# Layer 1 of two graph layers: three places for h, values of two tiles ago beside the transposes, source product over tanh, mask in two pieces

## The reference, cut to what matters

```python
h = jnp.einsum('bnd,ade->bane', feat_in, W)            # 12 heads of 64
th = jnp.tanh(h)
attn_src = jnp.einsum('bane,aeo->bano', th, w_src)
attn_dst = jnp.einsum('bane,aeo->bano', th, w_dst)
attn = attn_src + jnp.swapaxes(attn_dst, 2, 3)
attn = jnp.where(attn >= 0, attn, LEAKY_ALPHA * attn)
attn = jnp.where(~adj[:, None, :, :], jnp.float32(-999.0), attn)
attn = jax.nn.softmax(attn, axis=-1)
feat_out = jnp.einsum('banm,bame->bane', attn, h) + b
feat_out = jax.nn.elu(feat_out)                        # heads side by side
gate = jax.nn.sigmoid(feat_in @ H_w.T + H_b)
return gate * feat_out + (1.0 - gate) * feat_in        # then x + this, layernorm
```

## Time and profile before

| | us |
|---|---|
| median of 3 runs | 2741.1 |
| lowest, highest | 2740.21, 2742.04 |
| the profiled execution | 2743.32 |
| its span | 2741.6 |
| TensorE busy in the span | 2720.1 |
| VectorE busy | 1676.8 |
| ScalarE busy | 1211.7 |
| GpSimd busy | 926.6 |

### The profile page before, as it was taken

The page is one execution under the profiler, slowest core; times in us unless marked ns, Lnnn a source line. Parts: engine busy times, 40 slices in busy tenths (PEclk is TensorE's granted clock), DMA queues, the critical chain, the costliest instruction groups (busy, mean ns, idle before and its releaser), DMA issues.

```text
span 2741.6 us, 51890 instructions
## 1 busy us (share of the span) xinstructions
PE 2720.1 (99%) x20988; PEld 2513.6 (92%) x20988; DVE 1676.8 (61%) x3335; ACT 1211.7 (44%) x3109; POOL 926.6 (34%) x566
## 2 busy tenths in 40 slices
PE   8999999999999999999999999999999999999998
PEld 7777778878888899999999999999999999999998
DVE  7899998888888764444444444444544444444443
ACT  5666676666666743233332333233332333233332
POOL 2353334434444223323332333323332333323330
PEclk9999999999999999999999999999999999999999
DMA  6655665555555522222222222222232222222220
GB/s 186 171 137 145 164 158 143 140 140 140 137 141 139 189 65 67 73 82 71 59 82 70 72 69 67 73 82 71 59 82 71 80 61 68 73 82 71 59 70 24
DMA packets 306896, 269.50 MB, mean 98 GB/s; under 512 B 227809, under 2 KB 244193, under 8 KB 306657
## 3 DMA queue, kind: packets, MB, share of 16 engines
q1 hardware_dynamic: 306656, 266.19, 35.5%
HBM read 142.65 MB, written 75.89 MB: 80 GB/s over the span
## 4 chain that ended last, share of the span: by engine, by line
PE 88%; DVE 5%; DMA 3%; issue 2%; ACT 2%; SPq 1%; POOL 0%; DVEq 0%; ACTq 0%; POOLq 0%
PE ps_hg L1069 21%; PE ps_k L70 15%; PE ps_a L70 15%; PE ps_q L70 15%; PE ps_a L1244 15%; PE ps_s L1185 2%; PE ps_c L1210 2%; PE ps_pv L1101 1%; DMA dst_all<-dst_scratch 1%; ACT logits L567 1%; PE ps_t L1088 1%; PE ps_pt L1210 1%; DMA dst_scratch<-dst 1%; PE ps_pt L1192 1%; DVE logits L792 1%
## 5 line engine op out<-in xcount | busy, mean ns | idle before, releaser
L1069 PE MATMUL ps_hg<-w_hi,xT 128*128 128x512 f32 x2268 | 745.6, 401 | 4.5 <-DVE h_one L825 4.2
L1069 PEld LDWEIGHTS ps_hg<-w_hi,xT 128*128 128x128 f32 x2268 | 426.2, 188 | 108.1 <-issue 6.7
L1069 PE MATMUL ps_hg<-w_lo,xT 128*128 128x512 f32 x1134 | 448.4, 395 | 0.0
L70 PE MATMUL ps_k<-x1T_hi,wk_hi 128*128 128x256 f32 x1152 | 329.0, 286 | 0.0
L70 PE MATMUL ps_k<-x1T_lo,wk_hi 128*128 128x256 f32 x1152 | 321.8, 279 | 0.0
L70 PE MATMUL ps_k<-x1T_hi,wk_lo 128*128 128x256 f32 x1152 | 321.1, 279 | 0.0
L70 PE MATMUL ps_q<-x1T_hi,wq_hi 128*128 128x256 f32 x1140 | 319.3, 280 | 0.0
L70 PE MATMUL ps_q<-x1T_lo,wq_hi 128*128 128x256 f32 x1140 | 318.5, 279 | 0.0
L70 PE MATMUL ps_q<-x1T_hi,wq_lo 128*128 128x256 f32 x1140 | 317.8, 279 | 0.0
L497 POOL TENSOR_TENSOR th_src<-th,wsrc_all 128x768 f32<-128x768 f32 x64 | 118.3, 1849 | 479.9 <-DVE dst_all L805 462.1
L657 ACT ACTIVATE qT<-ps_q,bq_col 128x256 f32<-128x256 f32 x192 | 80.5, 470 | 451.6 <-PE ps_q L70 451.6
(11 more groups left out here) (156 smaller groups left out, 5747.3 us busy)
## 6 DMA issues: line engine op xcount, KB each, us to landing
x_tok<-x SPq DMA_DIRECT2D x64, 384.0 KB, 4.1
dst_all<-dst_scratch SPq DMA_DIRECT2D x128, 192.0 KB, 3.4
gate_scratch<-gate SPq DMA_DIRECT2D x64, 384.0 KB, 2.6
feat_scratch<-feat SPq DMA_DIRECT2D x128, 192.0 KB, 2.8
feat_in<-feat_scratch SPq DMA_DIRECT2D x62, 384.0 KB, 3.1
gate_in<-gate_scratch SPq DMA_DIRECT2D x62, 384.0 KB, 3.7
x_even<-x SPq DMA_DIRECT2D x16, 768.0 KB, 4.2
x_odd<-x SPq DMA_DIRECT2D x16, 768.0 KB, 4.4
```

Of the source, the lines that this page charges most:

```text
L70: ins = pe.matmul(out, left[a][c], right[b][c], start=(n == 0), stop=(n == len(terms) - 1))
L1069: ins = pe.matmul(ps_hg[:, cols], left[a][c], right[b][c], start=(c == 0 and n == 0), stop=(c == KC - 1 and n == 2))
```

## The change

`h_one` gets a third place, taken by `T % 3`; it lies where `th_src` lay, and GpSimd writes the source product over `th` instead. So `tanh_h(T)` waits for the sum over that product of T-1 (`src_done`), and GpSimd's wait for the sum goes. On TensorE `values(T-2)` moves behind `project(2, T)`, ahead of `transpose_probs(T-1)`. `attention`, the two exp steps and `elu` run three tiles behind in place of two, at the same place of a tile, and so do the stores of feat; the hand-over takes in the one left over. Mask and maximum are made in two pieces: the four heads of VectorE before the wait for ScalarE's Prelu, the eight of ScalarE behind it. Some SBUF offsets move by 64 bytes or so; `ones` lies over `att`.

```diff
-        th_src = at(S + 24576, "th_src", [P, D])
+        h_hole = at(S + 24576, "h_hole", [P, HEADS0, EW])
...
-        h_one = at(S + 36864, "h_one", [P, 2, HEADS0, EW])
+        h_one = [at(S + 36928, "h_one0", [P, HEADS0, EW]), h_hole, at(S + 40064, "h_one2", [P, HEADS0, EW])]
...
-                if 2 <= T < NT - 1:
-                    store_feat(T - 2)
+                if 3 <= T < NT - 1:
+                    store_feat(T - 3)
...
+            sp.wait_ge(pv_done, NT - 2)
             feat_and_gate(1, 0)
             for n in range(EARLY_W1, EARLY_W1 + KC):
                 load_chunk(sp, w1_chunks[n], w1_in[n])
+            store_feat(NT - 4)
             store_feat(NT - 3)
...
-                if T >= 1:
-                    pool.wait_ge(src_done, T)
-                pool.tensor_tensor(th_src[:, :], th[:, :], wsrc_all[:, :], ALU.mult).then_inc(thsrc_done, 1)
+                pool.tensor_tensor(th[:, :], th[:, :], wsrc_all[:, :], ALU.mult).then_inc(thsrc_done, 1)
...
                     act.wait_ge(thdst_done, T)
-                    act.wait_ge(thsrc_done, T)
+                    act.wait_ge(src_done, T)
                 act.activation(th[:, :], ps_hg[:, 0:D], ACT.Tanh).then_inc(tanh_done, 1)
...
                 exp_scores(T - 1)
-                if T >= 2:
-                    elu_exp(T - 2)
+                if T >= 3:
+                    elu_exp(T - 3)
...
             copy_probs(NT - 2)
+            elu_exp(NT - 3)
             act.wait_ge(cols_in, 48)
...
+            def masked_max(T, part, first, last):
+                n = last - first
+                scores_ = per_head(logits[:, first * NODES:last * NODES], n)
+                dve.copy_predicated(
+                    scores_, not_adj[:, T % 2, :].unsqueeze(1).to_broadcast([P, n, NODES]),
+                    masked[:, 0:1].unsqueeze(2).to_broadcast([P, n, NODES])).then_inc(masked_done, 1)
+                dve.wait_ge(masked_done, 2 * T + part + 1)
+                dve.tensor_reduce(neg_max[:, first:last], scores_, AX_X, ALU.max, negate=True).then_inc(max_done, 1)
...
-                dve.wait_ge(prelu_done, T + 1)
                 dve.wait_ge(leaky_done, T + 1)
                 dve.wait_ge(mask_done, T + 1)
-                dve.copy_predicated(
...
+                masked_max(T, 0, ON_ACT, HEADS0)
+                dve.wait_ge(prelu_done, T + 1)
+                masked_max(T, 1, 0, ON_ACT)
+                dve.wait_ge(max_done, 2 * (T + 1))
...
-                if T >= 2:
-                    dve.wait_ge(pv_done, T - 1)
-                dve.tensor_tensor(h_one[:, T % 2, :, 0:E0], per_head(ps_hg[:, 0:D], HEADS0),
+                if T >= 3:
+                    dve.wait_ge(pv_done, T - 2)
+                dve.tensor_tensor(h_one[T % 3][:, :, 0:E0], per_head(ps_hg[:, 0:D], HEADS0),
...
-                if T >= 2:
-                    attention(T - 2)
+                if T >= 3:
+                    attention(T - 3)
                 if T > 2:
                     bias_h(T)
                 if T == NT - 1:
                     bias_g(T)
+                    elu(T - 3)
                     break
                 src_scores(T)
                 bias_g(T)
-                if T >= 2:
-                    elu(T - 2)
+                if T >= 3:
+                    elu(T - 3)
...
+            attention(NT - 3)
+            softmax_scores(NT - 1)
             elu(NT - 3)
-            softmax_scores(NT - 1)
             attention(NT - 2)
...
                 project(1, T).then_inc(h_done, 1)
+                project(2, T).then_inc(g_done, 1)
                 if T >= 2:
                     values(T - 2)
-                project(2, T).then_inc(g_done, 1)
                 if T >= 2:
                     transpose_probs(T - 1)
```

More of the change, by code:

```diff
@@ L151, in two_graph_layers @@
         th = at(S + 21504, "th", [P, D])
-        th_src = at(S + 24576, "th_src", [P, D])
-        ones = at(S + 24576, "ones", [P, P])
-        Hb_less1 = at(S + 27648, "Hb_less1", [P, D])
-        dst_all = at(S + 30720, "dst_all", [P, D])
+        h_hole = at(S + 24576, "h_hole", [P, HEADS0, EW])
+        Hb_less1 = at(S + 27712, "Hb_less1", [P, D])
+        dst_all = at(S + 30784, "dst_all", [P, D])
         th_dst = dst_all
-        logits = at(S + 33792, "logits", [P, D])
+        logits = at(S + 33856, "logits", [P, D])
         probs = logits
-        h_one = at(S + 36864, "h_one", [P, 2, HEADS0, EW])
[L160 to L171, removed]
+        h_one = [at(S + 36928, "h_one0", [P, HEADS0, EW]), h_hole, at(S + 40064, "h_one2", [P, HEADS0, EW])]
+        probsT = at(S + 43200, "probsT", [P, HEADS0, NODES])
+        att = at(S + 46272, "att", [P, D])
+        ones = at(S + 46272, "ones", [P, P])
+        feat = at(S + 49344, "feat", [P, D])
+        gate = at(S + 52416, "gate", [P, D])
+        adj_u8 = at(S + 55488, "adj_u8", [P, 4, NODES], U8)
+        not_adj = at(S + 55744, "not_adj", [P, 2, NODES], U8)
+        dst = at(S + 55872, "dst", [P, HEADS0])
+        src = at(S + 55936, "src", [P, 2, HEADS0])
+        neg_max = at(S + 56032, "neg_max", [P, HEADS0])
+        row_inv = at(S + 56096, "row_inv", [P, 2, HB])
+        masked = at(S + 56160, "masked", [P, 1])
+        b_less1 = at(S + 56192, "b_less1", [P, E0])
         x1T_hi = at(S, "x1T_hi", [P, KC, GN], F32R)
@@ L788, in softmax_scores @@
                                          op0=ALU.mult, op1=ALU.max).then_inc(leaky_done, 1)
-                dve.wait_ge(prelu_done, T + 1)
                 dve.wait_ge(leaky_done, T + 1)
                 dve.wait_ge(mask_done, T + 1)
-                dve.copy_predicated(
-                    per_head(logits[:, :], HEADS0),
-                    not_adj[:, T % 2, :].unsqueeze(1).to_broadcast([P, HEADS0, NODES]),
-                    masked[:, 0:1].unsqueeze(2).to_broadcast([P, HEADS0, NODES])).then_inc(masked_done, 1)
-                dve.wait_ge(masked_done, T + 1)
-                dve.tensor_reduce(neg_max[:, :], per_head(logits[:, :], HEADS0), AX_X, ALU.max,
-                                  negate=True).then_inc(max_done, 1)
-                dve.wait_ge(max_done, T + 1)
+                masked_max(T, 0, ON_ACT, HEADS0)
+                dve.wait_ge(prelu_done, T + 1)
+                masked_max(T, 1, 0, ON_ACT)
+                dve.wait_ge(max_done, 2 * (T + 1))
                 dve.tensor_tensor(per_head(logits[:, :], HEADS0), per_head(logits[:, :], HEADS0),
@@ L830, in src_scores @@
                 dve.wait_ge(thsrc_done, T + 1)
-                dve.tensor_reduce(src[:, T % 2, :], per_head(th_src[:, :], HEADS0), AX_X, ALU.add).then_inc(src_done, 1)
+                dve.tensor_reduce(src[:, T % 2, :], per_head(th[:, :], HEADS0), AX_X, ALU.add).then_inc(src_done, 1)
             def bias_g(T):
@@ L890, in _ @@
             dve.memset(masked[:, :], MASKED0).then_inc(fixed, 1)
-            dve.memset(h_one[:, :, :, E0:EW], 1.0).then_inc(fixed, 1)
+            for place in h_one:
+                dve.memset(place[:, :, E0:EW], 1.0).then_inc(fixed, 1)
             rest_x(0)
@@ L895, in _ @@
             dve.wait_ge(memsets, 2)
-            dve.wait_ge(fixed, 2)
+            dve.wait_ge(fixed, 4)
             bias_h(0)
@@ L1101, in values @@
                             ins = pe.matmul(ps_pv[graph(half), g, k * EW:(k + 1) * EW], probsT[graph(g), a, :],
-                                            h_one[graph(g), T % 2, a, :], start=True, stop=True)
+                                            h_one[T % 3][graph(g), a, :], start=True, stop=True)
                 ins.then_inc(pv_done, 1)
```

2 lines of the change are left out of this document (1 added, 1 removed).

## The result

The changed kernel takes 2753.9 us (median of five executions; 2753.2 to 2756.0) against 2741.1 for the kernel before (median of five too; 2740.2 to 2742.0): a ratio of 1.0048, with an interval of 1.0036 to 1.0059. It is slower by some 13 us, above the range of 2731.5 to 2744. The profiled execution took 2753.59 us with a span of 2751.9, so it too has 1.7 us around its span, and the spans can be compared: 2751.9 less 2741.6 is +10.3 us.

The account below looks back on a forecast made before the run. TensorE, busy 99% of the span, was taken to bound the kernel. Terms -2.5 + 0.5 - 0.7 - 1.4 + 0.6 = -3.5 us took the median from 2741.1 to 2737.6 us; range 2731.5 to 2744.

Parts of the forecast that it names:

- the hand-over: Layer 1 to layer 2: tile 61's attention, exp and elu move in, delaying last exp and transposes; +0.6 us, 0 to +1.5.
- slower: Outcome of a measurement over 2746.6 us, said to be most of rival 3; chance 0.07.
- First tiles: TensorE's two early waits for h_one shrink, the second replaced by some 0.55 us for att; -1.4 us, -2 to 0.
- The meeting: Values and transposes side by side on TensorE save 0.04 us a tile over 62 tiles; -2.5 us, -3 to -1.
- rival 2: TensorE gains nothing because both tiling-mode drains are kept, and stalls only move; 2741 us, chance 0.12.
- The new wait of the values: Values on TensorE now need att from the same tile, with 0.01 us of slack; +0.5 us, 0 to 3.
- Rival 3: att is late in every tile, so values wait in each; slower, 2747.5 us at 0.16 us a tile; chance 0.09.
- The turns: Late dst-to-mask chains in tiles 10 to 25, VectorE full or DMA late, stall TensorE less; -0.7 us, -3 to +3.
- The DMA-bound ones: Six turns late through DMA, 14.7 to 15.4 us long, shortened by 0.55 each; they leave stalls of 1.25 us.
- The pieces: Mask and max in two pieces on VectorE: chain 0.55 us shorter where it waited for Prelu, +0.3 where not.
- rival 4: Third h place does nothing, only the pieces count; 2739 us, inside the forecast's 0.52.
- The source product: GpSimd writes it over tanh, so the next tanh waits for src; 8.6 us of cover, cost 0.

Follow-up runs that it names:

- The first two experiments: Changed kernel with the store of tile 60's feat moved on SP: right behind the loop, 2743.05 us; only ahead of the six weight loads, 2746.28 us.
- the first experiment: Changed kernel with the store of tile 60's feat issued on SP right behind layer 1's loop, ahead of everything: 2743.05 us, 1.0005 of before.
- its own pair of kernels: Attention at tile's end, load of x behind dst's write: 2738.67 us; same with values back between second and third projection: 2741.30 us.
- the two kernels with x behind and attention in the middle: Load of x moved behind dst's write, in the kernel before: 2742.69 us; in the changed kernel with tile 60's store ahead of everything: 2745.22 us.

## Why the prediction was wrong

**The step that failed is the hand-over: +0.6, "ends 0 and +1.5", measured +11.8, of which the store's place in SP's queue made 10.6.** I looked at the waits of the instructions that move in, attention, exp and elu of tile 61, on VectorE and ScalarE, and priced their length. I also looked at SP, but only downward, at what stands behind the stores; I named x_g[1] and the weights. I did not look at what elu_exp(61) waits for. Its wait for feat_stored of tile 60 stands two lines under its head, and the diff itself shows `store_feat(NT - 4)` put behind the load_chunk loop. In the trace of before the six loads at that place (from 937.18) took 3.1 us to issue, and a store behind them was harmless. With the upper end of that term at +10 in place of +1.5, "slower" would have had more than 0.07. The first two experiments show the cause: 12.8, 3.6 and 1.2 us above the kernel before as the store moves forward, with waits of 9.3, 2.6 and 0.6 us. Of the rest of the stretch, +1.2 in the first experiment with 0.6 of it the wait for exp, the term as I had meant it was right.

**First tiles: -1.4, measured +1.8 in tiles 1 to 3.** In the first half tile 2's start came 0.88 us sooner, counted from tile 1's (13.25 us in place of 14.13), against the 0.55. That is luck: the kernel with the mask in one piece and the one with the source product alone have 13.25 us there too, so the pieces did not bring it. The second half had the wrong price. att ended at 68.45 and the values started at 68.59, 0.25 ahead of the old start of tile 4. But what used to be done before the wait, values and transposes, now stood behind it: 1.49 us at full clock (615.35 to 616.84 in tile 41) and 2.70 here (68.59 to 71.29). -0.25 + 2.70 is the +2.45 at tile 4. I had set 0.55 of waiting against 1.4 and left out the work behind it, and the clock, which stood at 0.53 in 69.00 to 72.00, behind a stop of 3 us. The chain in tile 3 did not come sooner by att and elu either, since ScalarE waited for the DMA and not for VectorE:

```profile
60.38 2.52 ACT L567 ACTIVATE logits<-dst_all,src 128x64 f32<-128x64 f32 x8 [2.64 <-DMA dst_all<-dst_scratch]
```

With attention at the tile's end this loss is gone (tile 4 starts at 67.44), which bears this out.

**The meeting: -2.5, measured -2.6** by its own pair of kernels, and 0.048 us a tile in the trace where 0.04 was forecast. Right, and rival 2 with it refuted.

**The new wait of the values: +0.5.** From tile 27 on the stretch gained 1.23 us where 37 tiles of 0.048 are 1.78: +0.55. The slack of 0.01 held in most tiles; three tiles of that stretch were late, by 0.7 us in all. Rival 3, the one that ended slower, did not happen: the kernel became slower by another way, which I had not listed as one.

**The turns: -0.7, measured -1.9** (2.77 less 18 times 0.048). The one that I worked out most closely came as written: a stall of 1.5 behind the first mix, measured from 183.82 on as 1.44. Stalls of 0.4 and 0.7 follow; I had said 0.7, 0 and 0.4. The DMA-bound ones, 1.25 us in the forecast, were missing in this trace, but so they were in the trace of the source product alone. So part of this -1.9 may be the execution and not the change. One reason that I gave is contradicted: elu was to become shorter, and its mean rose from 1592 ns to 1847:

```profile
L853 DVE SCALAR_TENSOR_TENSOR feat<-att,feat 128x768 f32<-128x768 f32 x62 | 114.5, 1847 | 7.8 <-ACT feat L609 7.8
```

In tile 41 it took 2.00 us from 617.69, beside GpSimd's two copies, from 615.55 and 617.42, which had come forward with it.

**The pieces** did what was said of the chain (-0.57 in tile 41) but gave no measurable time alone, so rival 4 in the form of "only the pieces count, 2739" falls too: alone they gave 2742.95. **The source product** at 0 was right.

So without the misplaced store the change stands at 2743.05 against 2741.9: a gain of some 2.6 from the meeting, lost again in the first tiles, behind the mixes and in the hand-over (1.2 us in its trace). Two kernels came out under the kernel before, each by 0.1% with an interval that just clears 1: attention at the tile's end with the values where they were (2.4 us under it), and attention at the end with the meeting and the load of x moved (2.9). Both have attention at the end; by itself that isn't enough, as three more kernels have it and stand level with the kernel before or above it. With attention at the end the meeting gained 2.6 us where x was moved and lost 5.1 where it wasn't.

Still open: whether GpSimd's split beside the leaky maximum is all that eats the gain of moving x; why the values' place decides whether TensorE waits for h when dst's write is slow either way; and what makes the DMA-bound turns come and go.

## What to carry to other kernels

When a step moves to another place, go through each of its waits, also those for a free buffer, and follow each to the instruction that signals it and to its place in its own queue; here a store behind six large loads landed 8 us after its issue. A matmul block that is moved behind a wait costs, when the wait is late, the whole block and not the difference of the waits, and on top of it what the clock takes; in tile 3 that was 2.70 us against a wait that ended 0.25 sooner. Before a write that someone waits for, look at what stands just ahead of it in the same queue: one edit in the issuing order was worth 5.6 us here in one kernel, gave nothing in another and cost 2.2 and 2.5 us in two more, so it is to be measured in the place where it is meant to stay. And when a load moves, look at which engine's work starts behind it and what that work will then run beside.

## What the runs showed of the hardware

- A small write behind a large load in one queue, over tiles 4 to 59 of all fourteen traces: with the load of x (384 KB) issued less than 2 us ahead, the 6 KB took 2.8 us in the median (2.1 to 4.6); with it 3 us or more ahead 1.4 (1.4 to 3.3).
- The granted clock fell in stops of 3.0 and 9.3 us of TensorE: 0.53 in 69.00 to 72.00 and 0.51 in 951.00 to 956.00, after 1.00 in the tiles before. It fell too at stops of 2.0 us in tile 3 (the two kernels with x behind and attention in the middle), and did not at one of 2.6 us in the hand-over (the store ahead of the loads). The steps in the second stretch were twice as long as the 0.117 us of the earlier trace rows:

```profile
953.15 0.41 PE L70 MATMUL ps_q<-x1T_lo,wq_hi 128*128 128x256 f32 x1
953.37 0.41 PE L70 MATMUL ps_q<-x1T_hi,wq_lo 128*128 128x256 f32 x1
```

- Values (64x64 tiles) straight ahead of the transposes cost TensorE 0.04 to 0.05 us a tile less than the two apart, each between projections (14.26 against 14.31 us, and 2.6 us over 62 tiles).
- GpSimd's copy of 128x1536 uint16 beside VectorE's operation on 128x256 with two SBUF inputs: 1.5 to 1.7 us in place of 0.43.
- Splitting an operation on VectorE costs some 0.2 us: the predicated copy took 0.51 and 0.80 us in pieces against 1.09, the max 0.42 and 0.69 against 0.95.
